# Products of probabilities and values for four heads at a time, in every second group

## The reference

```
def _fq(x, delta, zp, n_bits):
    xi = _round_ste(x / delta) + zp
    xq = jnp.clip(xi, 0.0, 2.0 ** n_bits - 1.0)
    return (xq - zp) * delta

def _attn(x, ctx, wq, wk, wv, wo, bo, dq, dk, dv, dw):
    ...  # q, k, v = projections, split into 16 heads of 32
    sim = jnp.einsum('bhid,bhjd->bhij', _fq(q, dq, 128.0, 8), _fq(k, dk, 128.0, 8)) * SCALE
    attn = jax.nn.softmax(sim, axis=-1)
    out = jnp.einsum('bhij,bhjd->bhid', _fq(attn, dw, 0.0, 8), _fq(v, dv, 128.0, 8))
    out = out.transpose(0, 2, 1, 3).reshape(b, n, D)
    return out @ wo + bo

h1 = _ln(x, ln1_g, ln1_b)
x = _attn(h1, h1, ...) + x
h2 = _ln(x, ln2_g, ln2_b)
x = _attn(h2, context, ...) + x
```

## The kernel before

| step | fills of `two_` | step | fills of `one_` |
|---|---|---|---|
| 0 | q1 first half | 8 | transposes h2T, k2 first half |
| 1 | q1 second | 9 | q2 first |
| 2 | k1 first | 10 | q2 second |
| 3 | k1 second | 11 | k2 second |
| 4 | transposes ctxT, o1 first | 12 | o2 first |
| 5 | o1 second | 13 | o2 second |
| 6 | v1 first | 14 | v2 first |
| 7 | v1 second | 15 | transposes hT, v2 second |

## Time and profile before

### The profile page before, as it was taken

How to read it: one execution, slowest core, us unless ns; L and a number is a source line. 1 busy time by engine, 2 the same in 40 slices (tenths; PEclk the granted TensorE clock), 3 DMA queues, 4 the chain that set the end, 5 groups by cost and what they waited for, 6 DMA issues and landing times. The chain is left out here.

```text
span 2918.5 us, 55439 instructions
## 1 busy us (share of the span) xinstructions
PE 2712.4 (93%) x18432; PEld 2210.4 (76%) x18432; DVE 1783.6 (61%) x4410; ACT 1454.5 (50%) x3765; POOL 711.0 (24%) x1147
## 2 busy tenths in 40 slices
PE   5799999999999998489999999997999999999997
PEld 4566666666666665289999999997988888888885
DVE  6789999999999997554444443433444444444434
ACT  5577777777777775331111111112455555555554
POOL 1222222222222221132222232321221221222211
PEclk9899999999999999699999999999999999999999
DMA  4443333333333333431212111114111111111111
GB/s 149 82 82 83 83 79 83 80 83 81 85 84 83 79 83 56 114 128 57 79 50 79 65 65 69 61 72 137 51 44 49 52 43 50 50 43 50 50 36 44
DMA packets 337323, 211.07 MB, mean 72 GB/s; under 512 B 275568, under 2 KB 291952, under 8 KB 337264
## 3 DMA queue, kind: packets, MB, share of 16 engines
q1 hardware_dynamic: 337264, 210.34, 26.8%
HBM read 92.84 MB, written 50.33 MB: 49 GB/s over the span
## 5 line engine op out<-in xcount | busy, mean ns | idle before, releaser
L595 ACT ACTIVATE e<-S,bias,qk_scale 128x256 f32<-128x256 f32 x1024 | 563.1, 564 | 65.7 <-DVE e L707 61.6
L690 DVE TENSOR_REDUCE negmax<-S 128x4 f32<-128x1024 f32 x256 | 312.3, 1220 | 103.8 <-PE S L503 102.0
L707 DVE TENSOR_SCALAR e<-e,rsum 128x256 f16<-128x256 f32 x1024 | 292.0, 349 | 2.5
L565 ACT ACTIVATE shifted<-PJ,round_col,inv 128x512 f32<-128x512 f32 x192 | 149.2, 777 | 226.8 <-PE PJ L157 225.8
L148 PE MATMUL PJ<-w_a_wo,oT 128*128 128x512 f32 x512 | 239.3, 612 | 2.6 <-ACT oT L604 1.8
L1828 POOL TENSOR_TENSOR mid_partsB<-mid_actB,mid_partsB 128x256 fp32r<-128x256 f32 x128 | 97.9, 765 | 561.8 <-DVE mid_partsB L1664 561.8
L1828 POOL TENSOR_TENSOR mid_partsA<-mid_actA,mid_partsA 128x256 fp32r<-128x256 f32 x128 | 100.9, 788 | 518.2 <-DVE mid_partsA L1664 518.2
L157 PE MATMUL PJ<-hT,w_a_wq 128*128 128x256 f32 x1536 | 207.0, 293 | 21.3 <-DVE hT L685 17.5
L157 PEld LDWEIGHTS PJ<-hT,w_a_wq 128*128 128x128 f32 x1536 | 194.2, 197 | 35.3 <-issue 35.3
L157 PE MATMUL AG0B<-h_partsB,upB 128*128 128x256 f32 x1536 | 198.9, 286 | 16.1 <-DVE downB L1593 16.1
L595 ACT ACTIVATION_READ_ACCUMULATOR e<-S,bias,qk_scale 128x1 f32 x1024 | 208.8, 204 | 0.0
(11 more groups left out here) (198 smaller groups left out, 5471.0 us busy)
## 6 DMA issues: line engine op xcount, KB each, us to landing
x_in<-in_x_dram SPq DMA_DIRECT2D x16, 512.0 KB, 3.7
ctx_in<-in_ctx_dram SPq DMA_DIRECT2D x16, 512.0 KB, 3.6
mid_dram<-x SPq DMA_DIRECT2D x16, 512.0 KB, 2.7
y_in<-mid_dram SPq DMA_DIRECT2D x16, 512.0 KB, 3.3
kv_in<-in_ctx_dram SPq DMA_DIRECT2D x16, 512.0 KB, 3.4
h_dram<-h3TA SPq DMA_DIRECT2D x16, 512.0 KB, 2.6
k_dram<-k_out SPq DMA_DIRECT2D x16, 512.0 KB, 2.6
part_dram<-x3A SPq DMA_DIRECT2D x16, 512.0 KB, 2.6
```

Of the source, the lines that this page charges most:

```text
L565: nc.scalar.activation(shifted[:, bank, :], PJ[bank][:], ACT.Identity, bias=round_col[:, 0:1], scale=inv[:, d:d + 1]).then_inc(pj_emptied[ ...
L595: nc.scalar.activation(e[:, s, i, :], S[s][:, i // 2, i % 2, :], ACT.Exp, bias=bias[:, s, i:i + 1], scale=qk_scale[:, ph.a:ph.a + 1], accu ...
L690: nc.vector.tensor_reduce(negmax[:, g % 2, :], S[g % 2][:].rearrange("p i q n -> p (i q) n"), AX_X, ALU.max, negate=True).then_inc(max_don ...
L707: nc.vector.tensor_scalar(e16[:, s, i, :], e[:, s, i, :], rsum[:, s, i:i + 1], ROUND16, ALU.mult, ALU.add).then_inc(prob_scaled, 1)
```

## The change

PV is no longer done for two heads in every group but for four heads in every second one. `pe_pv` takes a quad (groups 2 x quad and 2 x quad + 1, heads 4 x quad to 4 x quad + 3) and waits for both transposed tiles. It issues eight matmuls: the first key half for the four heads, each in its own column tile, then the second key half for the four. It runs in even steps: quad g/2 - 2 in steps 4 and 6 of a phase, the last two quads of the phase before in steps 0 and 2. Semaphore `pv_done` goes up by 2. The number of matmuls, their shapes and what the other engines do stay.

```
-            def pe_pv(pe, ph, g):
-                pe.wait_ge(probs_turned[g % 2], turned_count(ph, g))
-                if g == 0:
+            def pe_pv(pe, ph, quad):
+
+                for g in (TT * quad, TT * quad + 1):
+                    pe.wait_ge(probs_turned[g % 2], turned_count(ph, g))
+                if quad == 0:
                     pe.wait_ge(quantised, ph.v_at)
-                half = g // (GROUPS // 2)
-                if g % (GROUPS // 2) == 0 and not (isinstance(ph.n, int) and ph.n == 0):
+                half = quad // 2
+                if quad % 2 == 0 and not (isinstance(ph.n, int) and ph.n == 0):
 
                     pe.wait_ge(oT_done, 2 * ph.n + half - 1)
-                for i in range(2):
-                    h = 2 * g + i
-                    r = DH0 * (h % 4)
-                    for kc in range(TT):
-                        ins = nc.tensor.matmul(O[half][r:r + DH0, (h // 4) % 2, :],
+                for kc in range(TT):
+                    for i in range(4):
+                        r = DH0 * i
+                        h = 4 * quad + i
+                        at = 4 * (i % 2) + kc
+                        ins = nc.tensor.matmul(O[half][r:r + DH0, quad % 2, :],
                                                vQ[ph.tiles][:, kc, h * DH0:(h + 1) * DH0],
-                                               pT[:, g % 2, 4 * i + kc:4 * i + kc + 3:2, :], start=(kc == 0),
-                                               stop=(kc == TT - 1))
-                ins.then_inc(pv_done, 1)
+                                               pT[:, i // 2, at:at + 3:2, :], start=(kc == 0), stop=(kc == TT - 1))
+                ins.then_inc(pv_done, 2)
...
-                    if g >= 3:
-                        pe_pv(pe, ph, g - 3)
-                    elif prev:
-                        pe_pv(pe, prev, g + GROUPS - 3)
+                    if g % 2 == 0 and g >= 4:
+                        pe_pv(pe, ph, g // 2 - 2)
+                    elif g % 2 == 0 and prev:
+                        pe_pv(pe, prev, g // 2 + 2)
...
-                for g in range(3):
-                    pe_pv(pe, ph, g + GROUPS - 3)
+                for quad in (2, 3):
+                    pe_pv(pe, ph, quad)
```

## The result

The changed kernel takes 2931.7 us in the median of 12 runs (2924.15 to 2941.8), the kernel before 2921.47 (2919.8 to 2926.82). The ratio is 1.0034, 95% interval 1.0022 to 1.0047: slower, where I had forecast 2905. The runs also lie further apart than before. The profiled run took 2935.76 us with a span of 2934.0.

What follows compares the result with a forecast made beforehand. In the quantised attention PE (busy 94%) and DVE (91%) were taken as the bound. -1.08 us a round over 14 rounds, -15.1, plus -1.0 in the phases outside gave -16.1: 2905 us, range 2894 to 2921.

Steps and rivals of the forecast that it cites:

- steps 7 and 15: Odd steps where PE waits for xhat (step 7's end) or turned (15): taking PV out saves nothing.
- clock rival: PE's clock falls in the fills of steps 8 and 15 as work leaves; about 2931 us; chance 0.09.
- step 9: Odd step after the k fill: -0.33 us in one round of two, mean -0.17.
- step 1: Odd step where PE has no idle time: 3.76 us becomes 3.39 without PV, so -0.37.
- steps 5 and 13: Odd steps with o fills: -0.33 us each, with DVE following.
- steps 3, 7, 11: Nothing saved: in 3 and 11 ACT is the bound; after 7 the xhat wait grows by 0.33 us.
- the block of eight: Joined PV block in even steps: next instruction starts after 0.35 us, +0.02 against the old block of four.
- serial rival: Column tiles in the PV block run one after another: block 1.1 us, total about 2970; chance 0.03.
- pairs-only rival: At most two column tiles run at once in the PV block: 0.57 us, total about 2925; chance 0.11.
- step 2: Even step: +0.02 us for the longer block; its transposed tile lands early enough to leave 0.05.
- landing rival: Transposed tiles come late in steps 2 and 10, so steps 1 and 9 save nothing; about 2913 us; chance 0.14.
- the transposes issued one step later: Even groups' transposes into pT wait for a later PV: delay 2.3 us, cover 5, so cost 0.

Runs made afterwards that it cites:

- all joined: The changed kernel as it is, with surplus PV matmuls added in PE's waits of steps 8 and 15: 2902.31 us.
- busy waits: Surplus PV matmuls in PE's waits of steps 8 and 15: kernel before 2910.15 us; changed kernel with group 4's products in steps 7 and 15, 2898.59.

## Why the prediction was wrong

**What failed.** The step on steps 7 and 15: "nothing; PV was inside a wait". With it the forecast left the low clock where it was, in every second fill of step 8 and in none of step 15. For the waits it holds (step 7 is 3.78 as before, step 15 without a slow fill 6.24). For the time it does not: those four matmuls were part of PE's work around a wait. Busy time by stretch, from the scores of step 8 and of step 15 to the fill behind the wait, before:

```profile
663.02:667.33 4.31, 1.82 (x17) 1.10 (x17) 4.25 (x11) 1.90 (x4) 1.78 (x3) 0.96 0.46 114
695.19:698.48 3.29, 1.81 (x18) 1.09 (x17) 2.68 (x5) 2.73 (x5) 0.20 (x1) 1.00 0.42 80
```

and after:

```profile
668.68:673.50 4.82, 2.84 (x21) 1.82 (x21) 3.89 (x10) 1.79 (x4) 1.78 (x3) 0.70 0.19 73
701.18:704.47 3.29, 1.48 (x13) 0.97 (x13) 3.00 (x6) 2.72 (x5) 0.20 (x1) 1.00 0.42 80
```

In step 15 PE does 1.81 us of work in 3.29 before, 1.48 in 3.29 after; the last line still has a clock of 1.00, and the slow stretch begins right behind it, at 704.77. In step 8 the slow stretch begins at 670.64, ahead of the transposes, instead of behind the products as at the earlier trace rows; so a slow step 8 costs 9.62 - 7.36 = 2.26 us and not 1.35. In the profiled run a slow step 8 came in 11 of the 14 rounds and a slow step 15 in nine; the forecast had seven and none.

The clock rival named this place and this mechanism, and its 2931 is what was measured. It had 0.09. That its sum fits is luck, by errors that cancel: a slow step 8 costs 2.26, not 1.35, and a slow step 15 1.59, not 1.35, but neither comes in all 14 rounds; and the saving without the clock is smaller than the 16.1 it starts from. I wrote against it that step 15 shows no slow fill in the kernel before. That is true, and it says little: there, the work was still in place. Yet with this work alone taken out step 15 has no slow fill either, and rounds 1 to 3 of the changed kernel have none: missing work is not enough by itself.

**What was right.** With the clock high in both, joining is worth 11.6 us with group 4's products left in steps 7 and 15 (2910.15 - 2898.59), and 7.8 with all joined (2910.15 - 2902.31). The second is the change as forecast; most of the difference is its round 0. My terms for such a round are -0.37 - 0.33 - 0.33 + 0.12 = -0.91 (step 9 gives back its gain in step 10, where the wait for pT grew: 3.85 to 4.27), 12.7 in 14 rounds; measured 0.86 and 0.84. Single terms, in us:
- step 1: -0.37, measured -0.37; steps 5 and 13: -0.33, measured -0.33;
- steps 3, 7, 11: nothing, measured nothing. But the wait for xhat did not grow to 2.3: it is 1.98 as before, and the 0.33 that PE has over stands in a wait of 0.30 for ACT ahead of the scores that open step 8;
- the block of eight: 0.35, measured 0.33. The serial and the pairs-only rival are out. The rule of the Trainium skill ("TensorE: Matmul & The Clock Gate", part 3, what overlaps and what doesn't), that weight loads overlap running matmuls only where row groups differ, does not hold for these column tiles: the block of eight was measured at 0.33 us, not at the 1.1 of the serial rival. All eight loads of the block that starts at 682.02 are over in 0.12 us, while its first matmuls still run (0.40 us in all for the block). The pairs of scores in the earlier trace rows that I took as the nearest rows are row tiles, not column tiles; the column pairs of that attention start 0.01 us apart too, so the 0.35 stands;
- step 2: no cost forecast, 0.05 left; with the clock high it costs 0.1, since its tile lands later than PE asks for it. The landing rival was right to that extent, and for step 10;
- step 12: +0.02 forecast, +0.1 measured, but not through the tile: with all joined and busy waits it landed at 605.58, before the scores at 605.89. The block has four waits ahead of it, all met by then, which PE's queue takes one after the other from 606.01 to 606.30. Before, the waits of this group stood in step 11, where ACT sets the pace;
- step 4: -0.12, not forecast. ACT's shifted of the fill before is earlier against PE, and the transposes wait less for it: 1.09 us busy instead of 1.29;
- the transposes issued one step later: no cost seen in rounds 1 to 12, where PE waits 1.4 us in all for pT, in step 10 of rounds 1 to 3. Round 0 is another matter: 1.55 us in step 2 and 1.39 in step 12. “pT waits on PE grow beyond step 10” and “slow fills appear in step 15” were two of my signs of being wrong, and both came.

**How sure.** Shown: work added inside the waits makes the changed kernel 21 to 29 us faster, and with both waits filled no slow fill is left in rounds 1 to 12; group 4's products taken out of steps 7 and 15 of the kernel before make it 5.6 us slower; work added elsewhere (step 1 and 9) also helps, by 12 us. So both count, what PE does around the waits and where the round falls. The Trainium skill ("TensorE: Matmul & The Clock Gate", part 1, what's actually happening) has the throttled state as the default that activity lifts. The busy waits agree: with both waits filled the granted clock was 1.00 throughout rounds 1 to 12, in three kernels. Open: by how much activity must drop in a wait, at which place, for the clock to fall; why single rounds are slow in one kernel and not in another; and why transposes land late in round 0. The spread of the changed kernel's runs (2924 to 2942) fits a varying number of caught rounds: the mean granted clock of the execution was 0.965 in the fastest run and 0.954 in the slowest. But only one run was profiled.

## What to carry to other kernels

Work inside a wait of PE is free by the chain of waits, but it may be what holds the clock. Before moving it out, look at the granted clock right behind each long wait; if some rounds already run at the low level there, price the change with the low level in all of them, and for all that follows. Surplus matmuls inside the waits of two steps were cheap: they took the changed kernel from 2931.7 to 2902.3 us, and its runs from 18 us apart (12 runs) to 2 (five).

## What the runs showed of the hardware that was not expected

- Four column tiles of 32 columns run together, whatever the order in which their matmuls are written: eight matmuls of 256 columns let the next instruction start after 0.33 us (key halves outermost) and 0.34 us (head by head). Two heads in the old order also took 0.33.
- Slow stretches repeat with the loop. In the changed kernel rounds 5 to 12 all took 71.6 to 71.7 us; with 0.7 us more work per round this no longer held. It can also end by itself: with the loops turned round, the same work, such rounds gave way to three of 68.4 to 68.5 us.
- PE doing more can take less time: +8 matmuls a round beside waits (steps 7 and 15) -22 us, +8 in steps that PE bounds -12 us.
